# Moving half of the last layer-three group between two products of the next chunk's layer two

## What is computed

```python
x = x + tanh(g_xattn) * xattn(layernorm(x), ctx, ctx)   # 16 heads, softmax over 128 keys
h = concatenate([y, -y]),  y = layernorm(x)
h = s0 * (h @ sign(k0));  h = relu(h) * 2               # layer one, 512 -> 2048
h = s1 * (h @ sign(k1));  h = relu(h) * 2               # layer two, 2048 -> 2048
h = s2 * (h @ sign(k2))                                 # layer three, 2048 -> 512
x = x + tanh(g_ffn) * h
```

## Time and profile before

| | us |
|---|---|
| median of 3 runs | 1574.0 (1572.46 to 1574.11) |
| the profiled execution | 1570.58 |
| its span, first to last instruction | 1568.8 |
| PE busy | 1523.2 (97%) |
| DVE busy | 938.5 (60%) |
| ACT busy | 672.3 (43%) |

### The profile page before, as it was taken

How to read it: one execution, slowest core, us unless ns; L and a number is a source line. 1 busy time by engine, 2 the same in 40 slices (tenths; PEclk the granted TensorE clock), 3 DMA queues, 4 the chain that set the end, 5 groups by cost and what they waited for, 6 DMA issues and landing times.

```text
span 1568.8 us, 46139 instructions
## 1 busy us (share of the span) xinstructions
PE 1523.2 (97%) x19872; PEld 1300.0 (83%) x19872; DVE 938.5 (60%) x1938; ACT 672.3 (43%) x1568; POOL 169.1 (11%) x273
## 2 busy tenths in 40 slices
PE   6798999999999999999999999999999999999998
PEld 4586888888988888898988888888898888889887
DVE  5877775656556565655656566465655656565441
ACT  3442342534535254452635445253553525345231
POOL 2202001020100202001020100101010010101000
PEclk9999999999999999999999999999999999999999
DMA  8443133242424334253442524333242432314100
GB/s 255 121 103 60 42 95 69 79 79 57 87 59 99 62 81 83 52 98 56 95 69 62 95 50 102 63 88 69 62 89 52 102 66 82 82 47 98 28 29 15
DMA packets 278227, 120.96 MB, mean 77 GB/s; under 512 B 243464, under 2 KB 259848, under 8 KB 277896
## 3 DMA queue, kind: packets, MB, share of 16 engines
q1 hardware_dynamic: 275960, 117.48, 34.6%
q10 hardware_dynamic: 2064, 0.53, 0.2%
HBM read 37.76 MB, written 16.78 MB: 35 GB/s over the span
## 4 chain that ended last, share of the span: by engine, by line
PE 87%; DVE 6%; ACT 3%; DMA 2%; issue 2%; SPq 0%; POOL 0%; DVEq 0%; ACTq 0%; POOLq 0%
PE bank L1252 22%; PE bank L1253 22%; PE bank L1219 7%; PE bank L1220 7%; PE bank L1269 6%; PE bank L1270 6%; PE bank L1136 2%; PE bank L1137 2%; PE bank L1138 2%; PE bank L1120 2%; PE bank L1121 2%; PE bank L1122 2%; ACT Pf L526 1%; PE bank L1164 1%; DMA PT<-Phl 1%
## 5 line engine op out<-in xcount | busy, mean ns | idle before, releaser
L1252 PE MATMUL bank<-H,W 128*128 128x128 f16 x6720 | 778.3, 219 | 8.3 <-ACT C L619 6.7
L1253 PE MATMUL bank<-H,W 128*128 128x128 f16 x6720 | 778.0, 219 | 0.0
L1252 PEld LDWEIGHTS bank<-H,W 128*128 128x128 fp8e5 x6720 | 655.3, 98 | 20.8 <-ACT C L619 12.3
L1253 PEld LDWEIGHTS bank<-H,W 128*128 128x128 fp8e5 x6720 | 657.4, 98 | 7.1
L1219 PE MATMUL bank<-hT,W 128*128 128x256 f16 x1024 | 226.8, 273 | 3.5 <-DVE hT L742 1.9
L1220 PE MATMUL bank<-hT,W 128*128 128x256 f16 x1024 | 226.8, 272 | 0.0
L526 ACT ACTIVATE Pf<-bank,nmax 128x128 f32<-128x128 f32 x512 | 145.9, 368 | 139.1 <-DVE nmax L801 137.4
L1269 PE MATMUL bank<-W,h 128*128 128x512 fp8e5 x512 | 194.0, 379 | 1.6 <-DVE h L849 1.6
L1270 PE MATMUL bank<-W,h 128*128 128x512 fp8e5 x512 | 194.0, 379 | 0.0
L473 POOL TENSOR_TENSOR attn<-pvs 128x128 f32<-128x128 f32 x120 | 75.6, 630 | 1002.8 <-DVE pvs L814 1002.8
L841 DVE TENSOR_TENSOR C<-bank,C 128x256 f32<-128x256 f32 x180 | 76.2, 423 | 161.8 <-ACT C L619 89.9
(11 more groups left out here) (129 smaller groups left out, 1911.3 us busy)
## 6 DMA issues: line engine op xcount, KB each, us to landing
Qst<-q_bounce SPq DMA_DIRECT2D x120, 128.0 KB, 2.8
Y<-in_x_dram SPq DMA_DIRECT2D x16, 512.0 KB, 3.8
R<-X SPq DMA_DIRECT2D x16, 512.0 KB, 3.5
q_bounce<-Qhl SPq DMA_DIRECT2D x120, 64.0 KB
out_dram<-R SPq DMA_DIRECT2D x15, 512.0 KB, 2.7
W<-in_L_ffn_k_dram SPq DMA_DIRECT2D x8, 512.0 KB, 8.2
W<-in_L_ffn_k_dram SPq DMA_DIRECT2D x2, 1024.0 KB, 18.7
PT<-Phl SPq DMA_TRANSPOSE x120, 3.1
```

Of the source, the lines that this page charges most:

```text
L1252: mm(o, w, H0[:, 0, i, b_of, :], start=first, stop=False, skip_group_check=True)
L1253: last = mm(o, w, H0[:, 1, i, b_of, :], start=False, stop=i == PAIRS - 1, skip_group_check=True)
```

## The change

Half 1 of `"L2P"` leaves slot 9 and stands in group 0 between P7 and P4, as slot 14. So P1, P2, P6, P5 and P7 of group 0 move up by one slot (9 to 13), while the woven items and the weight steps keep their slot numbers. The `finish` of DVE, the store by SP, and in chunk 0 the load of group 2's weights are bound to the second `"L2P"` and go with it. SP's wait for the store with the copy of X moves from slot 12 to P1 of group 1, slot 17.

```diff
-    SLOTS = [("L0", i, 0) for i in range(PAIRS)] + [("L2P", GROUPS - 1, h) for h in range(2)]
+    SLOTS = [("L0", i, 0) for i in range(PAIRS)] + [("L2P", GROUPS - 1, 0)]
     for q in range(GROUPS):
         SLOTS += [("L1", q, s) for s in (P1, P2, P6, P5, P7)]
-        SLOTS += [("L2", q - 1, h) for h in range(2)] if q else []
+        SLOTS += [("L2", q - 1, h) for h in range(2)] if q else [("L2P", GROUPS - 1, 1)]
         SLOTS += [("L1", q, s) for s in (P4, P3)]
...
-                    if f and slot == ("L1", 0, P6):
+                    if f and slot == ("L1", 1, P1):
                         sp.wait_ge(out_stored, nth(f - 1, 16, 15))
                         keep_x1(f)
```

## The result

The changed kernel takes 1579.47 us (median of 12 runs) where the kernel before, run on the same chip, takes 1572.59 (12 runs): a ratio of **1.0044, interval 1.0035 to 1.0053**, or 5.5 to 8.3 us more. One of the changed kernel's 12 executions took 1753.3 us at a granted clock of 0.849; the ratio leaves it out, and the median of the other eleven is 1579.29. The change makes the kernel slower by more than 0.2%. The prediction gave 1579.4 with +5.4 us. That the two times agree to 0.1 us is luck: over 12 runs the kernel before is 1.4 us faster than the three runs had it on which the prediction was built, and the difference came out 1.5 us larger than predicted.

The account below looks back on a forecast made before the run. PE and the hand-over chain of DVE and ACT were taken as nearly equal bounds. Terms -0.4 - 0.2 + 4.9 + 1.1 = +5.4 us took the median from 1574.0 to 1579.4 us, range 1574.0 to 1584.5.

Parts of the forecast that it names:

- What bounds the kernel: Chunks 2 to 14: PE and the DVE-ACT hand-over chain bound nearly equally; PE loses 0.41 us at P4, 0.2 at P6.
- the second, smaller stop at P6: Group 1, each chunk: PE could start P6 at 594.14 but waits for a take until 594.33, 0.2 us lost.
- PE's part: Group 0, chunks 2 to 14: the moved half covers P4's wait for the take; taken alone -0.41 us a chunk.
- The chain: DVE and ACT, chunks 2 to 14: 2.1 us added against 1.72 won, +0.38 a chunk, together +4.9 us; chance 0.60.
- P1 without its cover: Group 0's P1 reaches layer one's last pair just in time, 0 to 0.1 us a chunk; chunk 15 waits, +1.1.
- The first two chunks: Chunk 1: a weight step leaves DVE's chain, -0.2 us. Chunk 0: DVE's chain starts a little earlier, -0.4 us.
- Transfers: SP's moved store and copy of X beside transposing transfers: between 0 and perhaps 0.3 us a chunk, taken as 0.
- The sum: Whole kernel: all terms together +5.4 us, median 1574.0 to 1579.4 us, 0.34% slower.
- PE alone: Rival, chunks 2 to 14: DVE's chain has room, the 0.41 us is won; -4.8 us, 1569.2; chance 0.10.
- The cancelling case: Rival, chunks 2 to 14: PS 1 or the finish costs 0.25 us less a chunk; +2.2 us, 1576.2; chance 0.16.
- The colliding transfers: Rival: store and copy delay PV 3 or PV 4 by 0.3 to 0.5 us a chunk; 1583.5 to 1586; chance 0.14.

Follow-up runs that it names:

- the finish in slot 17: Changed kernel with DVE's finish moved behind the scaling of PV 1, store at slot 17 and copy of X at slot 20; 1563.1 us, ratio 0.9943.
- the finish alone: Kernel before with only DVE's finish, SP's store and copy of X at the new places, the half of layer three unmoved; 1592.09 us, ratio 1.0127.
- the woven items earlier: Changed kernel with S0, PS0, S1, PS1 and the third query load one slot earlier in all chunks; 1573.4 us, ratio 1.0002.
- the transfers alone: Kernel before with only SP's store and copy of X moved to the new places; 1572.75 us, ratio 1.0004.
- the half finish: Changed kernel with only the first finish instruction behind the half of layer three, the second behind the scaling of PV 1; 1569.8 us, ratio 0.9988.
- early load: Changed kernel with SP issuing group 2's weights in chunk 0 at slot 9, as before; one execution, 1582.22 us.

## Why the prediction was right

**What bounds the kernel.** Right, and the second, smaller stop at P6 was needed: the finish in slot 17 wins 0.62 to 0.64 a chunk, not 0.41, because both stops of the earlier trace rows were of one chain.

**PE's part.** P4's stop is gone, as said (586.61 to 586.83).

**The chain.** All times of the chunk shown lie 1.21 behind the prediction's, which is what had gathered by then (P1 575.50 for 574.29). With that taken off, the chain's events are: take 583.87 (said 583.87), rest of C22 585.20 (585.19), maximum 587.65 (587.64), rest of P4 589.81 (589.80), P1 590.30 (590.29), P6 594.74 (594.71). The step was said to be 0.38 and is 0.39. The two terms inside it are shown apart: 1.32 of the finish by the finish alone and by the slot 17, 0.76 of `PS` 1 by the woven items (they take 0.79 off both chain and step, 0.03 more than said).

**P1 without its cover.** Said 0 in the chunks 2 to 14. In the chunk shown P1 of group 0 runs through its pairs without a wait. In chunk 15 "about 2 us": 1.36 and 0.87 between neighbouring starts, and +1.1 for the chunk in the trace, as said.

**The first two chunks.** Chunk 1: said -0.2, is -0.18. Chunk 0: said -0.4, is -0.10. This is the term that was mis-sized, inside its bounds of -0.7 and +1, and its mechanism was wrong: I had let DVE's long chain start a little earlier, but its first weight step starts later. The woven items keep their slot numbers, so one more product stands ahead of the first scores. Before:

```profile
97.15 1.28 DVE L980 TENSOR_SCALAR W<-W,w_mask 128x2048 uint32<-128x2048 uint32 x1
```

And after:

```profile
99.38 1.28 DVE L980 TENSOR_SCALAR W<-W,w_mask 128x2048 uint32<-128x2048 uint32 x1
```

Less the 0.50 that lie before the chunk, that is 1.73 later. DVE catches up because two of its waits in before's trace, 1.42 at 107.48 and 1.26 at 109.99, are not in the profile after, which has one of 1.33 in this stretch. First use of group 2's weights is at 116.28; less 0.50 this is 115.78, only 0.18 earlier than in the earlier trace rows. That the chunk ends 0.10 early and not late is luck as far as the prediction goes.

**Transfers.** Said 0, and the transfers alone give 1.0004. The rule of the Trainium skill (page "DMA: Bandwidth & Descriptors", section "Issuing engines are not separate DMA queues") that all transfers interleave on the same engines gives no size, and the traces are compatible with it: of the 104 transposing transfers of the chunks 2 to 14, 28 took more than 3.6 us to land before and 26 after. Moving store and copy among them changed which are slow (in the chunk shown the first took 4.4 before and 3.4 after) and not, measurably, how many, nor how long PE waits.

**The sum.** +5.4 against a measured +6.9 (5.5 to 8.3), so slightly small, just below the interval. Of the 6.96 in the trace, 0.50 before chunk 0 and 0.6 of varying waits for transfers are put down to the execution. For the rest, 5.9, the terms give 5.4; 0.3 of the gap is chunk 0, and most of the rest is the 0.01 between 0.38 and 0.39, 13 times. In the times another part that is too small is probably chunk 15, as the last section says. That is argued from traces and not shown: of a timed run the record has the granted clock of the whole span alone, 0.994 to 0.999 in the eleven of the changed kernel, and this does not say where in the span it fell.

**The rivals.** PE alone (-4.8) needed at most 1.3 us in the chain; the finish in slot 17 shows that with 0.79 this rival is what happens, and more. The cancelling case needed 0.25 less chain, and the half finish (0.66 less) goes through it to the other side. The colliding transfers are ruled out.

## What to carry to other kernels

When an instruction is moved past others, list for every engine what goes with it; here 1.72 us of PE moved well and 1.32 us of DVE that had cost nothing moved into a chain of hand-overs and was paid in full. A stop of the busiest engine is won only up to what the chain behind the next stop allows, so follow the chain past the first stop to the point where the engine catches up. An order that is right for the middle of a loop needs a look at the first and the last pass: the same reordering gave -0.40 in each of 13 passes and lost all of it in three others. (Part of that loss, 1.6 us in the last pass, was a lower clock that the trace of another kernel with the same stop does not have.)

## What I had not expected of the hardware

The same stop of PE costs two different prices. In chunk 15 P1 waits in all kernels with the half moved in the same two steps. In the profile after it is followed by full clock; the columns are the stretch, its length, busy time and count of each engine, the granted clock, the share of the DMA engines and GB/s:

```profile
1508.00:1510.00 2.00, 2.00 (x39) 2.00 (x37) 0.64 (x2) 0.42 (x1) 0.00 (x0) 1.00 0.03 8
```

In the kernel with the woven items earlier the waits have the same lengths and the clock is then 0.50, which is 1.2 in place of 2.4 GHz:

```profile
1499.10 0.23 PE L1253 MATMUL bank<-H,W 128*128 128x128 f16 x1 [1.19 <-DVE H L837]
...
1500.21 0.23 PE L1253 MATMUL bank<-H,W 128*128 128x128 f16 x1 [0.71 <-DVE H L837]
```

```profile
1502.00:1504.00 2.00, 2.00 (x21) 2.00 (x20) 0.42 (x1) 0.00 (x0) 0.00 (x0) 0.50 0.03 8
```

21 matmuls in 2 us where the other has 39. Chunk 15 takes 2.7 more there, not 1.1, so the lower clock costs 1.6. Of the traces with the half moved in chunk 15, two have 1.1 (after, finish in slot 17) and three have 2.7 (woven items earlier, half of the finish, early load). Putting the last chunk back won 2.4 us in one pair of kernels (1.0044 to 1.0029) and 2.0 in the other (0.9943 to 0.993), between the two prices, as if the clock fell in a part of the executions; the intervals overlap in both pairs, so this is a guess. That the same order can meet a fall at different places is shown further ahead in the kernel: in the changed kernel the granted clock is 0.50 from 143 to 145 (chunk 0) and 1.00 from 223.5 to 226 (chunk 1), and in the kernel that differs from it in chunk 15 alone it is 1.00 in the first stretch and 0.50 in the second. What decides when it falls was not tried.
